# Counting ten one-hot columns: one VectorE sum in place of four additions

## The chip, the cores and the metric

The kernel runs on one core of one Trainium2 chip. The metric is the device time of one execution in microseconds. The engines are TensorE (PE), VectorE (DVE), ScalarE (ACT), GpSimd (POOL), and SyncE (SP), which issues plain DMAs.

## What is computed

One block of a graph transformer over N = 6250 rows of 256 values, with E = 106250 weighted edges. In the reference, cut to what matters:

```python
xn = layernorm(x)
low  = relu(segment_sum(val_low[:, None]  * (xn @ W_low)[dst],  src, N))   # GNN, two edge weights
high = relu(segment_sum(val_high[:, None] * (xn @ W_high)[dst], src, N))
mlp  = relu(xn @ W_mlp)
x = x + 3 * attention_mix(low, high, mlp) + linear_attention_mixer(xn)
y = layernorm(x);  weights = y @ wr
x = x + y + (ffn(y) * weights on the 3124 rows of largest weight, else 0)
```

The segment sum needs the edges grouped by `src`. The kernel does a counting sort of its own on the chip, into 98 buckets of 64 rows each (`src >> 6`), and this sort is where the change lies.

## The kernel before

Three stages follow one another. **The sort** (some 30 us to 765 us of the execution) takes the edges in 28 batches of 30 columns by 128 partitions, and runs beside it, tile quad by tile quad, the layer norm and key/value sums (slots 0 to 12), a folding of weights (slot 13), and the mixer (slots 14 to 24, with two quads left for after the last batch). **The gather stage** (some 765 us to 1835 us) fetches for every sorted column of 128 edges the rows of `xn` (852 indirect DMAs from GpSimd, line 665), multiplies them by selection matrices on TensorE, and runs attention, second layer norm and feed-forward tile by tile. **The end** finds the threshold of the largest weights and stores.

Every engine has its own instruction stream, all written out in the same order by `schedule` (line 372 on), which calls a function `slot(g, ...)` of each engine once a slot. Between engines there are semaphores only. In slot g VectorE does, in this order: the variance of the quad before; `pick_rank(g)` (line 766: 30 x 98 products of one-hots and ranks) and `place(g)` (lines 776 and 778 to 790: positions); key/value scaling, or in the mixer's slots `mix_out`; `one_hot(g+1)` (line 733: `oh`, for each of 128 partitions 30 columns of 98 buckets, bf16); `sum_hots(g+1)` (lines 746 to 752, the part that is changed); `cells(g)` and `cell_records(g)` (lines 794 to 808: operands of the permuting matmuls); layer-norm moments; `destinations(g-1)` (lines 824 and 826: where the records of batch g-1 go); `find_ties(g+1)`; `step_mask(g)`; the layer norm's apply.

`oh` is laid out [30 columns][98 buckets], so one column's 98 one-hots are contiguous and the same bucket of the next column lies 98 bf16 values, 196 bytes, further. The 30 columns make 3 groups of 10. `sum_hots` counts, in each partition and group, how many of the ten columns fall into each bucket: 3 x 98 counts. It does so by halves: columns 0-4 plus 5-9, then two plus two, then one plus one, then the odd fifth. Each addition waits for the one before through the semaphore `many_set`.

The counts go to TensorE's `ranks(g+1)`, its last work in slot g: it waits for `many_set` and for `idx_ready` of batch g-1, and multiplies the counts by triangles of ones into ranks. ScalarE copies these (`copy_rank`, line 1310), and VectorE's `pick_rank(g+1)` waits for that copy at the head of the next slot. GpSimd's `scatter(g)` (line 648) waits for `rec_staged` of ScalarE and for `idx_ready`, which line 826 on VectorE sets, and issues 16 indirect DMAs for the batch; index and record buffers are double, so VectorE's line 824 and ScalarE's line 1319 wait for the scatter of two batches before. The gather stage begins once all scatters have landed. Of the tile `many`, only `many[:, :, 0, :]` is read by TensorE.

Of the kernel before, what the change touches and what calls it, by code (L numbers as in the profile page):

```python
# [17 lines left out]
BF16 = mybir.dt.bfloat16  # L18
ALU = mybir.AluOpType
ACT = mybir.ActivationFunctionType  # L20
AX = mybir.AxisListType

P = 128
# [5 lines left out]
GS = 10  # L29
GROUPS = BB // GS  # L30
# [13 lines left out]
def wait(eng, sem, value):  # L44

    if isinstance(value, int) and value <= 0:
        return
    eng.wait_ge(sem, value)


def build(nc, a, out):
# [5 lines left out]
    NB = 2 * T  # L57
# [41 lines left out]
    with ExitStack() as ctx:  # L99
        sems = {}  # L100

        def S(name):
            if name not in sems:
                sems[name] = ctx.enter_context(nc.semaphore(name))
            return sems[name]

        def sb(name, shape, dt=F32):
            return ctx.enter_context(nc.sbuf_tensor(name, shape, dt))
# [37 lines left out]
        r1 = Region(0)  # L146
# [14 lines left out]
        oh = r1.take([P, BB, NB], BF16)  # L161
# [7 lines left out]
        quots = [base[:, spare:T * D].rearrange("p (j q) -> p j q", q=P), side[:, spare:T * D].rearrange("p (j q) -> p j q", q=P),  # L169
                 r1.take([P, GS, P])]  # L170
        iota_q = r1.take([P, STEPS], U16)
        many = r1.take([P, GROUPS, GS // 2, NB], BF16)
        iota32 = r1.take([P, P])
        earlier = r1.take([P, GS, GS], BF16)
        before_f = r1.take([P, P])
# [144 lines left out]
        ones_b = sb("ones_b", [P, P], BF16)  # L320
        before = sb("before", [P, P], BF16)
# [354 lines left out]
        def _(dve):  # L676
# [62 lines left out]
            def sum_hots(g):  # L739

                dve.wait_ge(S("oh_set"), g + 1)
                wait(dve, S("rank_ready"), g)
                h = oh[:, :, :].rearrange("p (s j) b -> p s j b", s=GROUPS)
                H = GS // 2
                with nc.allow_low_precision(reason="whole numbers up to ten"):
                    dve.tensor_tensor(many[:, :, :, :], h[:, :, 0:H], h[:, :, H:GS], ALU.add).then_inc(S("many_set"), 1)
                    dve.wait_ge(S("many_set"), 4 * g + 1)
                    dve.tensor_tensor(many[:, :, 0:2], many[:, :, 0:2], many[:, :, 2:4], ALU.add).then_inc(S("many_set"), 1)
                    dve.wait_ge(S("many_set"), 4 * g + 2)
                    dve.tensor_tensor(many[:, :, 0], many[:, :, 0], many[:, :, 1], ALU.add).then_inc(S("many_set"), 1)  # L750
                    dve.wait_ge(S("many_set"), 4 * g + 3)
                    dve.tensor_tensor(many[:, :, 0], many[:, :, 0], many[:, :, 4], ALU.add).then_inc(S("many_set"), 1)

            def find_ties(g):

# [14 lines left out]
            def place(g, par):  # L770

                dve.wait_ge(S("prod_set"), g + 1)
                dve.wait_ge(S("ties_set"), g + 1)
                H = (NB + GS) // 2
                with nc.allow_low_precision(reason="whole numbers below 2 ** 13, one of a bucket's and at most nine ties"):
                    dve.tensor_tensor(prod[:, :, 0:H], prod[:, :, 0:H], prod[:, :, H:2 * H], ALU.add).then_inc(S("prod_half"), 1)
                    dve.wait_ge(S("prod_half"), g + 1)
                    dve.tensor_reduce(posi[:, :], prod[:, :, 0:H], AX.X, ALU.add).then_inc(S("pos_set"), 1)
                dve.wait_ge(S("pos_set"), g + 1)
# [117 lines left out]
            def slot(g, par, kv, ln, post, mix, mixed):  # L897
# [15 lines left out]
                if more:  # L913
                    one_hot(g + 1)
                    sum_hots(g + 1)
# [125 lines left out]
            dve.tensor_reduce(hcnt[0:M, :, :].rearrange("p b k -> p (b k)"), hsel[0:M, :, :], AX.X, ALU.add).then_inc(S("hist_split"), 1)  # L1041
            one_hot(0)
            sum_hots(0)
            dve.wait_ge(S("counts_ready"), 1)
            step(dve.tensor_copy(cnt_i[0:NR, :], bank[6][0:NR, 0:G]))
# [234 lines left out]
            for n, (t0, t1) in enumerate(OUT):  # L1280
                if n == 0:
                    dve.wait_ge(S("y_ready"), t1)
                    for i in range(t0, t1):
                        ins = dve.scalar_tensor_tensor(base[:, i * D:(i + 1) * D], side[:, i * D:(i + 1) * D], mask[:, i:i + 1],
                                                       base[:, i * D:(i + 1) * D], ALU.mult, ALU.add)
                else:
                    dve.wait_ge(S("y_masked"), n)
                    ins = dve.tensor_tensor(base[:, t0 * D:t1 * D], base[:, t0 * D:t1 * D], side[:, t0 * D:t1 * D], ALU.add)  # L1288
# [234 lines left out]
        def _(pe):  # L1523
            def mm(out_, lhsT, rhs, start, stop, **kw):
                return pe.matmul(out_, lhsT, rhs, start=start, stop=stop, **kw)  # L1525


            def ranks(g):

                pe.wait_ge(S("many_set"), 4 * g + 4)  # L1530
                wait(pe, S("idx_ready"), 1 if isinstance(g, int) and g == 1 else g - 1)
                R = bank[0][:, 0:RANKS]
                mm(R, ones_f[0:NB, :], diag[0:NB, :].unsqueeze(1).to_broadcast([NB, GROUPS, NB]), True, False, skip_group_check=True)
                mm(R, before[:, :], many[:, :, 0, :], False, False, skip_group_check=True)
                for s in range(GROUPS - 1):
                    ins = mm(R[:, (s + 1) * NB:], ones_b[:, :], many[:, s:s + 1, 0, :].to_broadcast([P, GROUPS - 1 - s, NB]),
                             False, s == GROUPS - 2, skip_group_check=True)
                ins.then_inc(S("rank_ready"), 1)

# [3 lines left out]
            for g in range(G):  # L1543
                if g % (G // 2) == 0:
                    pe.wait_ge(S("digits_ready"), (H1 + H2) * (1 + g // (G // 2)))
                for u in range(BB // HG):
                    c = g * (BB // HG) + u
                    ins = mm(bank[2 + g // PER][0:M, (g % PER) * W:(g % PER + 1) * W], oh1[:, c * M:(c + 1) * M], oh2[:, c * W:(c + 1) * W],
                             u == 0, u == BB // HG - 1)
# [3 lines left out]
            for k in range(H2):  # L1553
                ins = mm(bank[6][0:NR, 0:G], spread[0:M, k, :, :].rearrange("p h k -> p (h k)"), hcnt[0:M, :, k], k == 0, k == H2 - 1)
            ins.then_inc(S("counts_ready"), 1)
            pe.wait_ge(S("runs_ready"), 1)
            mm(bank[6][0:NR, 32:32 + G], before_f[0:NR, 0:NR], runs[0:NR, :], True, True).then_inc(S("lpos_ready"), 1)
            pe.wait_ge(S("diag_ready"), 1)
            ranks(0)
            pe.wait_ge(S("totals_ready"), 1)  # L1560
            mm(bank[6][0:NR, 64:65], before_f[0:NR, 0:NR], incl[0:NR, G - 1:G], True, True)
# [123 lines left out]
            def slot(g, par, kv, ln, post, mix, mixed):  # L1685
# [53 lines left out]
                if more:  # L1739
                    ranks(g + 1)  # L1740
# [12 lines left out]
            for k in range(NBLK):  # L1753
# [6 lines left out]
                for f in range(4):  # L1760
                    ins = pe.transpose(bank[k][:, f * P:f * P + n], by_field[:, f, :], ident[0:n, 0:n])
# [151 lines left out]
```

## Time and profile before

| | us |
|---|---|
| median of 3 runs | 1971.31 (1970.63 to 1973.62) |
| the profiled execution's own time | 1968.29 |
| its span in the profile | 1966.5 |
| VectorE busy in the span | 1239.8 (63%) |
| GpSimd busy | 1376.8 (70%) |
| TensorE matmul busy | 1567.2 (80%) |

Busy time is the sum of instruction durations on an engine. Line numbers are those of the kernel. In a row of the timeline the first number is the start, the second the duration, and a bracket at the end says how long the engine sat idle before it and who ended that. An instruction's recorded duration can overlap by some tens of nanoseconds with the next one on its engine that does not wait for it, so what a step costs its engine is read from start to start.

### The profile page before, as it was taken

How to read it: one execution, taken by the hardware profiler on the slowest of the kernel's cores; microseconds unless marked ns; L12 is line 12 of the kernel's file. 1: busy time of each engine (PE TensorE's matmuls, PEld its weight loads, DVE VectorE, ACT ScalarE, POOL GpSimd, SP SyncE). 2: the span in 40 equal slices, each digit the busy share in tenths (PEclk: the TensorE clock that was granted, in tenths of full speed). 3: DMA queues.
4: the chain of work that ended last, by engine and by line, in shares of the span. 5: the costliest groups of instructions: out<-in, count | busy, mean ns of one | idle time of the engine just before them, and what ended most of it. 6: DMA issues, size and time to landing. Idle time of an engine off the chain costs nothing.

```text
span 1966.5 us, 30490 instructions
## 1 busy us (share of the span) xinstructions
PE 1567.2 (80%) x9109; PEld 1327.7 (68%) x9109; DVE 1239.8 (63%) x3136; ACT 915.6 (47%) x2641; POOL 1376.8 (70%) x1351
## 2 busy tenths in 40 slices
PE   3788888599998561788889888888888888889871
PEld 3466666588877561577777777777777777777750
DVE  8899999879988730345544554455454545545546
ACT  1688888677877550133333343333333334333323
POOL 4337778777777776777777777777777777777700
PEclk9899999789999785799999999999999999999975
DMA  3222221111121003433333333333333333333303
GB/s 89 83 66 68 68 68 49 40 36 47 48 66 47 6 6 95 133 102 105 100 102 103 104 101 105 105 101 100 102 103 103 102 103 105 100 102 105 103 14 131
DMA packets 102212, 162.99 MB, mean 83 GB/s; under 512 B 32190, under 2 KB 72762, under 8 KB 102040
## 3 DMA queue, kind: packets, MB, share of 16 engines
q0 software_dynamic: 55232, 113.59, 20.6%
q1 hardware_dynamic: 46808, 47.29, 7.6%
q8 instruction: 85, 1.39, 0.3%
q14 instruction: 87, 0.71, 0.1%
HBM read 139.76 MB, written 21.04 MB: 82 GB/s over the span
## 4 chain that ended last, share of the span: by engine, by line
POOL 31%; issue 13%; DMA 9%; DVE 2%; PE 2%; SPq 2%; ACT 1%; DVEq 0%; POOLq 0%; ACTq 0%
POOL arena L665 31%; DMA arena<-xn_rows,arena 9%; PE bank L1525 2%; SPq L558 1%; ACT side L1516 1%; POOL sorted_records L648 1%; DVE arena L1246 0%; DVE arena L1248 0%; DVE arena L1119 0%; DVE arena L1113 0%; SPq L563 0%; SPq L561 0%; DVE base L1288 0%; DVE arena L1253 0%; DVE arena L1245 0%
## 5 line engine op out<-in xcount | busy, mean ns | idle before, releaser
L1525 PE MATMUL bank<-arena 128*128 128x128 f32 (+3 forms) x6320 | 1145.1, 338 | 146.8 <-DVE arena L1119 74.4
L1525 PEld LDWEIGHTS bank<-arena 128*128 128x128 f32 (+1 forms) x6320 | 982.5, 188 | 287.8 <-issue 143.2
L665 POOL DMA_INDIRECT arena<-xn_rows,arena x852 | 840.7, 987 | 267.1 <-issue 246.1
L648 POOL DMA_INDIRECT sorted_records<-arena x448 | 512.9, 1145 | 218.0 <-issue 138.0
L1119 DVE TENSOR_TENSOR arena<-arena 128x640 f32<-128x640 bf16 (+1 forms) x204 | 164.4, 806 | 29.1 <-DVE arena L1113 0.2
L1113 DVE SCALAR_TENSOR_TENSOR arena<-io,arena 128x320 bf16<-128x320 f32 (+1 forms) x204 | 97.6, 479 | 96.5 <-issue 44.4
L1164 DVE CUSTOM_DVE_ANT_0 arena<-arena 128x256 f32<-128x256 f32 x98 | 37.8, 423 | 166.2 <-ACT arena L1449 166.2
L1169 DVE SCALAR_TENSOR_TENSOR att_prod<-sg,att_neg 128x9 f32<-128x9 f32 x49 | 8.4, 171 | 212.0 <-ACT sg L1457 212.0
L1525 PE MATMUL bank<-arena,base 128*128 128x128 f32 (+3 forms) x766 | 118.0, 287 | 22.0 <-ACT base L1304 13.8
L1525 PEld LDWEIGHTS bank<-arena,base 128*128 128x128 f32 (+2 forms) x766 | 110.2, 212 | 23.2 <-ACT base L1304 14.4
L1487 ACT ACTIVATE arena<-bank 128x256 f32<-128x256 f32 x49 | 18.8, 383 | 228.6 <-PE bank L1525 228.6
L808 DVE TENSOR_TENSOR arena<-arena 128x1280 f32<-128x1280 bf16 x84 | 120.3, 1488 | 1.0
L1435 ACT ACTIVATE arena<-bank,b1f 128x128 f32<-128x128 f32 x392 | 106.1, 385 | 5.0 <-PE bank L1525 5.0
L1465 ACT ACTIVATE nr<-nri 128x1 f32<-128x1 f32 x49 | 9.9, 203 | 203.1 <-DVE nri L1194 203.1
L1525 PE MATMUL bank<-side,arena 128*128 128x512 f32 x196 | 100.9, 641 | 0.0
L1300 ACT ACTIVATE base<-arena 128x128 f32<-128x128 f32 x280 | 84.8, 388 | 19.3 <-DVE arena L789 19.3
L1300 ACT ACTIVATE arena<-arena 128x128 f32<-128x128 f32 x280 | 84.7, 399 | 0.0
L1300 ACT ACTIVATE side<-arena 128x128 f32<-128x128 f32 x280 | 84.6, 395 | 0.0
L1449 ACT ACTIVATE arena<-bank 128x512 f32<-128x512 f32 x49 | 29.3, 597 | 102.2 <-PE bank L1525 102.2
L1440 ACT ACTIVATE arena<-bank 128x256 f32<-128x256 f32 x49 | 18.8, 383 | 123.9 <-PE bank L1525 123.9
L1525 PE MATMUL bank<-arena,side 128*128 128x128 f32 x560 | 67.7, 276 | 0.1
L766 DVE TENSOR_TENSOR arena<-arena 128x2940 f16<-128x2940 bf16 x28 | 47.3, 1689 | 32.0 <-ACT arena L1310 31.9
(311 smaller groups left out, 1918.2 us busy)
## 6 DMA issues: line engine op xcount, KB each, us to landing
arena<-xn_rows,arena POOLq DMA_INDIRECT x852
sorted_records<-arena POOLq DMA_INDIRECT x448
arena<-in_x SPq DMA_DIRECT2D x12, 512.0 KB, 4.1
xn_rows<-arena SPq DMA_DIRECT2D x12, 512.0 KB
x_plus_xn_rows<-arena SPq DMA_DIRECT2D x12, 512.0 KB
arena<-x_plus_xn_rows SPq DMA_DIRECT2D x12, 512.0 KB, 3.9
arena<-xn_rows SPq DMA_DIRECT2D x12, 512.0 KB
out<-base SPq DMA_DIRECT2D x4, 1024.0 KB
```

What stands on the lines that cost most here:

```text
L558: word = sp.value_load(free_word[group:group + 1, 0:1], min_val=1, max_val=2 ** 19 - 1)
L648: pool.indirect_dma_start(rec_dram, bass.IndirectOffsetOnAxis(ap=idx[0:PR, par, u:u + 1], axis=0), stage_rec[0:PR, par, u * 8:(u + 1) * 8] ...
L665: pool.indirect_dma_start(gring[:, c % GR, :], None, xn_dram, bass.IndirectOffsetOnAxis(ap=rring[:, c, 3:4].bitcast(I32), axis=0)).then_in ...
L766: dve.tensor_tensor(prod4[:, :, :, 0:NB], oh[:, :, :].rearrange("p (s j) b -> p s j b", s=GROUPS), rankf[:, :].rearrange("p (s b) -> p s b ...
L808: dve.tensor_tensor(cellrec[:, t, :].rearrange("p t (f c) -> p t f c", f=4), cell[:, t, :].unsqueeze(2).to_broadcast([P, GS, 4, GC]), raw[ ...
L1113: return dve.scalar_tensor_tensor(out_, io64[:, :].unsqueeze(1).to_broadcast([P, n, BK]), float(BK * b), r[:, :, 0:1].to_broadcast([P, n, ...
L1119: return dve.tensor_tensor(out_, hots.unsqueeze(2).to_broadcast([P, n, 2, BK]), r[:, :, 1:3].unsqueeze(3).to_broadcast([P, n, 2, BK]), ALU ...
L1164: ins = dve.tensor_tensor_reduce(out=lg_prod[:, k, :], in0=lh[:, k * D:(k + 1) * D], in1=att_rows[:, k, :], scale=1.0, scalar=0.0, op0=ALU ...
L1300: ins = act.activation(quot[:, j, :], iota32[:, :], ACT.Abs, bias=p32[:, par, s * GS + j:s * GS + j + 1], scale=-1.0)
L1435: act.activation(fh[:, f, :], bank[4 + part][:, (f % 4) * P:(f % 4 + 1) * P], ACT.Gelu_apprx_tanh, bias=b1f[:, f:f + 1]).then_inc(S("fh_re ...
L1449: act.activation(lh[:, :], bank[3][:, :], ACT.Relu).then_inc(S("lh_ready"), 1)
L1525: return pe.matmul(out_, lhsT, rhs, start=start, stop=stop, **kw)
```

## The change

The four additions of `sum_hots` become one `tensor_reduce` over a view of `oh` whose innermost axis runs along the ten columns of a group. The tile `many` shrinks to the 3 x 98 counts, and TensorE's `ranks` reads it directly and waits for one increment a batch where there were four. All 28 batches are changed. Nothing else is; the layer-normed rows are computed on VectorE as before.

```diff
--- before.py
+++ after.py
@@ -169,7 +169,7 @@
         quots = [base[:, spare:T * D].rearrange("p (j q) -> p j q", q=P), side[:, spare:T * D].rearrange("p (j q) -> p j q", q=P),
                  r1.take([P, GS, P])]
         iota_q = r1.take([P, STEPS], U16)
-        many = r1.take([P, GROUPS, GS // 2, NB], BF16)
+        many = r1.take([P, GROUPS, NB], BF16)
         iota32 = r1.take([P, P])
         earlier = r1.take([P, GS, GS], BF16)
         before_f = r1.take([P, P])
@@ -740,16 +740,8 @@
 
                 dve.wait_ge(S("oh_set"), g + 1)
                 wait(dve, S("rank_ready"), g)
-                h = oh[:, :, :].rearrange("p (s j) b -> p s j b", s=GROUPS)
-                H = GS // 2
                 with nc.allow_low_precision(reason="whole numbers up to ten"):
-                    dve.tensor_tensor(many[:, :, :, :], h[:, :, 0:H], h[:, :, H:GS], ALU.add).then_inc(S("many_set"), 1)
-                    dve.wait_ge(S("many_set"), 4 * g + 1)
-                    dve.tensor_tensor(many[:, :, 0:2], many[:, :, 0:2], many[:, :, 2:4], ALU.add).then_inc(S("many_set"), 1)
-                    dve.wait_ge(S("many_set"), 4 * g + 2)
-                    dve.tensor_tensor(many[:, :, 0], many[:, :, 0], many[:, :, 1], ALU.add).then_inc(S("many_set"), 1)
-                    dve.wait_ge(S("many_set"), 4 * g + 3)
-                    dve.tensor_tensor(many[:, :, 0], many[:, :, 0], many[:, :, 4], ALU.add).then_inc(S("many_set"), 1)
+                    dve.tensor_reduce(many[:, :, :], oh[:, :, :].rearrange("p (s j) b -> p s b j", s=GROUPS), AX.X, ALU.add).then_inc(S("many_set"), 1)
 
             def find_ties(g):
 
@@ -1527,13 +1519,13 @@
 
             def ranks(g):
 
-                pe.wait_ge(S("many_set"), 4 * g + 4)
+                pe.wait_ge(S("many_set"), g + 1)
                 wait(pe, S("idx_ready"), 1 if isinstance(g, int) and g == 1 else g - 1)
                 R = bank[0][:, 0:RANKS]
                 mm(R, ones_f[0:NB, :], diag[0:NB, :].unsqueeze(1).to_broadcast([NB, GROUPS, NB]), True, False, skip_group_check=True)
-                mm(R, before[:, :], many[:, :, 0, :], False, False, skip_group_check=True)
+                mm(R, before[:, :], many[:, :, :], False, False, skip_group_check=True)
                 for s in range(GROUPS - 1):
-                    ins = mm(R[:, (s + 1) * NB:], ones_b[:, :], many[:, s:s + 1, 0, :].to_broadcast([P, GROUPS - 1 - s, NB]),
+                    ins = mm(R[:, (s + 1) * NB:], ones_b[:, :], many[:, s:s + 1, :].to_broadcast([P, GROUPS - 1 - s, NB]),
                              False, s == GROUPS - 2, skip_group_check=True)
                 ins.then_inc(S("rank_ready"), 1)
 
```

## Rows read from the trace of the kernel before

**Rows 1.** The page, parts 1, 2 and 4.

```profile
PE 1567.2 (80%) x9109; PEld 1327.7 (68%) x9109; DVE 1239.8 (63%) x3136; ACT 915.6 (47%) x2641; POOL 1376.8 (70%) x1351
...
DVE  8899999879988730345544554455454545545546
...
POOL 4337778777777776777777777777777777777700
...
POOL 31%; issue 13%; DMA 9%; DVE 2%; PE 2%; SPq 2%; ACT 1%; DVEq 0%; POOLq 0%; ACTq 0%
```

**Rows 2.** Windows: one batch of each half (stretch, length, busy time per engine).

```profile
299.91:324.43 24.52, 21.99 (x145) 17.13 (x144) 23.79 (x50) 20.29 (x54) 19.64 (x17) 0.93 0.17 50
489.23:509.59 20.36, 20.15 (x145) 17.98 (x145) 19.65 (x30) 17.20 (x44) 16.09 (x15) 1.00 0.20 56
```

**Rows 3.** Timeline of VectorE (start, us taken): the four additions and what follows.

```profile
309.44 0.92 DVE L746 TENSOR_TENSOR arena<-arena 128x1470 bf16<-128x1470 bf16 x1
310.40 0.47 DVE L748 TENSOR_TENSOR arena<-arena 128x588 bf16<-128x588 bf16 x1
310.90 0.31 DVE L750 TENSOR_TENSOR arena<-arena 128x294 bf16<-128x294 bf16 x1
311.25 0.32 DVE L752 TENSOR_TENSOR arena<-arena 128x294 bf16<-128x294 bf16 x1
311.48 0.21 DVE L794 CAST arena<-arena 128x60 bf16<-128x60 int32 x1
```

**Rows 4.** Instructions by line on VectorE, whole trace: busy us, mean ns.

```profile
L778 DVE TENSOR_REDUCE arena<-arena 128x30 int32<-128x1620 f16 x28 | 51.6, 1841 | 1.0
...
L746 DVE TENSOR_TENSOR arena<-arena 128x1470 bf16<-128x1470 bf16 x28 | 26.2, 935 | 1.0
...
L1248 DVE TENSOR_REDUCE arena<-arena 128x15 f32<-128x735 f32 x8 | 7.4, 919 | 0.3
```

**Rows 5.** Timeline of VectorE: two sums of one tile, strided and contiguous.

```profile
17.82 0.29 DVE L707 TENSOR_REDUCE base<-base 128x6 f32<-128x78 f32 x1
18.03 0.23 DVE L708 TENSOR_REDUCE base<-base 128x13 f32<-128x78 f32 x1
```

**Rows 6.** Instructions of line 711, VectorE: ns min/median/max, starts, forms.

```profile
L711 DVE COPY base<-base x8: 163/168/566, 18.3 to 19.4; 128x12 f32<-128x12 f32 x6, 128x13 f32<-128x13 f32 x2
```

**Rows 7.** Timeline of VectorE: batch 0, first addition and what follows the fourth.

```profile
30.83 1.21 DVE L746 TENSOR_TENSOR arena<-arena 128x1470 bf16<-128x1470 bf16 x1
...
34.27 0.18 DVE L1045 CAST base<-bank 104x28 int32<-104x28 f32 x1
```

**Rows 8.** Timeline of VectorE: the products by rank, and the idle time before them.

```profile
299.91 1.68 DVE L766 TENSOR_TENSOR arena<-arena 128x2940 f16<-128x2940 bf16 x1
...
385.13 0.92 DVE L746 TENSOR_TENSOR arena<-arena 128x1470 bf16<-128x1470 bf16 x1
...
402.49 1.69 DVE L766 TENSOR_TENSOR arena<-arena 128x2940 f16<-128x2940 bf16 x1 [0.92 <-ACT arena L1310]
...
424.64 1.69 DVE L766 TENSOR_TENSOR arena<-arena 128x2940 f16<-128x2940 bf16 x1 [5.78 <-ACT arena L1310]
...
509.59 1.69 DVE L766 TENSOR_TENSOR arena<-arena 128x2940 f16<-128x2940 bf16 x1 [0.23 <-ACT arena L1310]
```

**Rows 9.** Timeline of VectorE and GpSimd: the handover of batch 14.

```profile
443.20 0.17 DVE L826 TENSOR_TENSOR arena<-arena,bank 128x16 int32<-128x16 f32 x1
...
444.17 1.43 POOL L648 DMA_INDIRECT sorted_records<-arena  x1 [3.06 <-DVE arena L826]
```

**Rows 10.** Windows of line 648 alone (scatters on GpSimd).

```profile
444.00:765.40 321.40, 248.75 (x224) 0.88 0.14 37
...
720.00:765.00 45.00, 34.33 (x36) 0.73 0.13 27
```

**Rows 11.** Timeline of VectorE: slot 26, which has no mixer work.

```profile
669.58 1.69 DVE L766 TENSOR_TENSOR arena<-arena 128x2940 f16<-128x2940 bf16 x1 [2.96 <-ACT arena L1310]
...
684.18 0.17 DVE L824 TENSOR_TENSOR arena<-bank,arena 128x16 f32<-128x16 f32 x1
```


## The prediction, made before the changed kernel ran

> **What bounds the kernel now.** I read the page first, for which stage the change touches and who is busy in it. The 40 slices are of 49 us each: VectorE stands at 8 or 9 tenths from the first slice to the tenth, the sort, and near half afterwards, where the chain that ended last is made mostly of GpSimd's gathers [rows 1]. The change is in the sort alone, and the gathers wait for its last scatter. So the question is what moves that scatter.
>
> Next I read two stretches of one batch each [rows 2]. In the first half of the sort a batch takes 24.52 us and VectorE has 23.79 of them; the rest is starts, not waiting: the timeline shows no idle bracket before its instructions. It is the bound. In the second half a batch takes 20.36 us and VectorE has 19.65; the one wait is 0.23 us at the head of the slot for ScalarE's copy of the ranks [rows 8]. TensorE has 20.15 us there, but its `ranks` waits for line 826 of VectorE, so the ring runs VectorE, TensorE, ScalarE, VectorE, and a longer VectorE slot makes the ring longer. From batch 14 on a third party counts. GpSimd waits 3.06 us for line 826 of VectorE and starts at 444.17 [rows 9]; from there to 765.4 it issues 224 scatters, 14 batches, 22.96 us each [rows 10]. That is slower than VectorE's 20.36, so VectorE gets ahead and GpSimd sets the end.
>
> In short: up to 443 us every microsecond on VectorE moves the end by one. After that only what makes its slot longer than about 23 us does.
>
> **What it removes.** The four additions take 2.04 us of VectorE, from the start of the first (309.44) to the start of line 794 (311.48), their waits on each other included [rows 3]. In batch 0 they take 3.44 us, 30.83 to 34.27, since some are slower there [rows 7].
>
> **What it adds.** One sum over 2940 bf16 values with 294 results. Two sums over contiguous values give the rate: 1620 values take 1841 ns and 735 take 919 ns, so (1841 - 919) / 885 = 1.042 ns a value and 153 ns fixed. The first of them reads f16, so 16-bit values bring no double rate in this row. An addition of 1470 bf16 values takes 935 ns, about half a nanosecond a value over the same fixed part [rows 4]. The floor for the sum is therefore 2940 x 1.042 + 153 = 3.22 us.
>
> But those rows step from one value to its neighbour. Here the innermost step is 196 bytes. One pair of rows in the trace shows what a step can cost: lines 707 and 708 sum the same 78 f32 values, 707 with an innermost step of 24 bytes and 708 along the row: 293 ns against 226 [rows 5]. The 67 ns are 0.86 ns a value, nearly one more tick of 1.042 ns each. In line 711, which writes 12 values at a step of 32 bytes, the median is 168 ns, only some 15 ns over the fixed part of the sums [rows 6]; this speaks neither for nor against a price on reads. I take the row of the same operation. Scaled by values, 2940 x 0.86 = 2.53 us more, 5.75 us in all. If a full tick is added to each value and the short sum hid its first dozen, it is 2940 x 2.084 + 153 = 6.28 us. Floor 3.22, ceiling 6.28; I take 6.0, between the two readings of the nearest row. Like line 752 it overlaps its successor by 0.09 us [rows 3], so it costs 5.91 from start to start, and a batch gets **5.91 - 2.04 = 3.87 us** longer on VectorE.
>
> The Trainium skill, SBUF — State Buffer, section "Door 1: The DMA port swizzle", says that SBUF is read in lines of 16 bytes and that each access which crosses to a new line pays a penalty. The trace agrees as far as it goes, by the 67 ns of line 707; the page gives no price.
>
> **Edits at no cost.** TensorE reads the counts from 294 contiguous values where it read three runs of 98; it has the same columns, and one semaphore count a batch in place of four costs VectorE only what the 2.04 us already contain. No DMA, no queue and no PSUM bank is touched. GpSimd's scatters take 1.11 us each while VectorE works (248.75 / 224) and 0.95 us in the last stretch with hardly any (34.33 / 36) [rows 10], 2.5 us a batch for all of VectorE's work. If the additions had their share, 2.04 of 20 us, their absence would give GpSimd back 0.26 us a batch, 3.6 us over 14 batches; what the sum takes from it instead is unknown. I count zero and keep 4 us either way.
>
> **Where the 3.87 us land.** Behind the sum on VectorE stand lines 794 to 808, whose cells TensorE permutes in the next slot, and lines 824 and 826, for which both TensorE's `ranks` and GpSimd wait.
> - Batch 0: 5.91 - 3.44 = +2.5 us, before anything overlaps it.
> - The sums of batches 1 to 14, the last at 385.13 [rows 8]: 14 x 3.87 = +54.2 us. The weight folding in slot 13 is a dialogue of VectorE and TensorE and is only moved.
> - The sum in slot 14 (402.49 to 424.64): VectorE idles 5.78 us before the next batch's products [rows 8], for TensorE's mixer work. This covers 3.87 us: 0. Without that cover it would be one more 3.87.
> - The sum in slot 15 stands ahead of line 826 at 443.20, for which GpSimd waits [rows 9]: +3.9 us. Batch 14 is handed over 60.6 us later, at 503.8.
> - From slot 16 VectorE needs 20.36 + 3.87 = 24.23 us a batch, GpSimd 22.96. So GpSimd waits for VectorE again. To line 826 of slot 26 there are 11 slots, the last 3.8 us shorter (14.60 us from line 766 to 824 [rows 11], where in slots with mixer work three more instructions, 3.8 us, come between): 11 x 24.23 - 3.8 = 262.7, batch 25 at 766.5, GpSimd's start 1 us later, 767.5.
> - Batches 25 to 27 are then GpSimd's again: with VectorE thinning out, between 20.0 us (45.00 / 36 x 16) and 22.96 us each [rows 10], 65.5 us for the three. The last scatter ends at 833.0 where it ended at 765.4.
>
> The gather stage and the end move as they are. Sum: **+67.6 us** on the profiled execution's 1968.3, which gives 2035.9. That execution stands 3.0 us under the median of the runs shown, so I predict 1971.3 + 67.6 = **2039 us**. With a sum of 5.75 us the same steps give +61 to +62 (2033), with 6.28 us +75 (2046).
>
> **Rivals.**
> *The step costs nothing.* Then the sum takes 3.22, a batch gets 3.13 - 2.04 = 1.09 us longer. Batch 0 gains 0.3, batches 1 to 14 lose 15.3, slot 15 loses 1.1; then the VectorE slot is 21.45 us, under GpSimd's 22.96, and after one more handover, which is just in time today, nothing is added: +17, **1988 us**. For it: line 711, and that the 67 ns are one single instruction. Against it: lines 708, 778 and 1248 lie within 10 ns of one line, 707 does not. The Trainium skill, VectorE: DVE Perf Modes, section "Mode 1× (REGULAR) — the baseline", has one result a cycle whatever the stride; by that rule this rival holds, and the 67 ns of line 707 contradict it here.
> *The sum reads bf16 in pairs.* The place is the sum itself: at two values a tick it takes 2940 x 0.521 + 153 = 1.69 us, 1.60 from start to start, 0.45 us under the additions. It decides for a gain once the sum is shorter than 2.13 us. 15 batches give back 6.7 us, batch 0 another 1.8, and GpSimd's pace swallows the rest: -8.5, **1963 us**. For it: the additions do read at that rate. Against: the f16 sum of line 778 does not, and pairs along a step of 196 bytes are not neighbours.
> *GpSimd covers it.* If its rate counted from the first batch, nothing would change (1971). Against: it waits for line 826 up to batch 14 [rows 9].
>
> **How the numbers follow.** The step costs: 0.70. It costs nothing: 0.23. Pairs: 0.05. Cover or a chance meeting near zero: 0.02. Against a measurement that can tell 0.2% (4 us): slower 0.93, same 0.02, faster 0.05. Range: the likeliest case runs from 2033 to 2046, with 4 us for GpSimd 2029 to 2050; to leave out no more than 2 in 10 it must reach down to the second case, less the 4 us: 1984 to 2050.
>
> **What will show it.** In the changed profile one sum of 2940 values on VectorE near 6.0 us (3.2: the first rival; under 2.1: the second). Batches of the first half 28.4 us apart at line 766. An idle time of GpSimd before each batch's scatter after 500 us, ended by line 826; about 1.9 us of idle time left before line 766 after slot 14. A last scatter near 833 us and a gather stage as long as before. I am wrong if the sum's duration is outside 5.7 to 6.3 us, or if the slots of the second half stretch by less than the sum does.

## The result and the profile after

| | before | changed |
|---|---|---|
| median, us | 1972.39 (1970.63 to 1973.62, 4 runs) | 2033.38 (2026.91 to 2035.38, 4 runs) |
| ratio | | 1.0304, 95% interval 1.0279 to 1.0329 |
| span of the profiled execution | 1966.5 | 2031.8 |
| last scatter issued (line 648) | 764.2 | 820.9 |
| first and last gather issued (line 665) | 771.5, 1872.1 | 828.3, 1938.1 |

The kernel is 61 us slower; forecast were 67 (2039, range 1984 to 2050). The page of the changed kernel, the lines that answer to [rows 1]:

```profile
PE 1593.4 (78%) x9109; PEld 1350.0 (66%) x9109; DVE 1327.7 (65%) x3052; ACT 915.4 (45%) x2641; POOL 1396.0 (69%) x1351
...
DVE  8899999989999991145544554554455545555446
...
POOL 31%; issue 12%; DMA 9%; DVE 2%; PE 2%; SPq 2%; ACT 1%; DVEq 0%; POOLq 0%; ACTq 0%
```

VectorE stands at 8 or 9 tenths in each of the first 15 slices, of 51 us now, where before, in slices of 49 us, it stood so in 12 of the first 13; it has 84 instructions fewer (3052 against 3136) and 88 us more work. The chain that ended last is GpSimd's as before.

The timeline of VectorE round one sum, which answers to [rows 3] (start, us taken), and below it all 28 sums of line 744 (ns min/median/max, first and last start):

```profile
342.62 5.25 DVE L744 TENSOR_REDUCE arena<-arena 128x294 bf16<-128x2940 bf16 x1
347.79 0.18 DVE L786 CAST arena<-arena 128x60 bf16<-128x60 int32 x1
```

```profile
L744 DVE TENSOR_REDUCE arena<-arena x28: 5067/5222/5294, 30.8 to 740.0; 128x294 bf16<-128x2940 bf16 x28
```

The sum takes 5.25 us here and 5.17 us from its start to the next start. The additions took 2.04. Batch 0, which answers to [rows 7]:

```profile
30.80 5.09 DVE L744 TENSOR_REDUCE arena<-arena 128x294 bf16<-128x2940 bf16 x1
...
35.80 0.19 DVE L1037 CAST base<-bank 104x28 int32<-104x28 f32 x1
```

5.00 us where it was 3.44: +1.6 us. Two stretches of one batch each, which answer to [rows 2] (stretch, length, busy time of PE, PEld, DVE, ACT, POOL):

```profile
332.91:360.53 27.62, 23.22 (x145) 18.59 (x144) 27.00 (x47) 20.15 (x54) 19.35 (x17) 0.87 0.15 45
518.90:542.31 23.41, 21.78 (x146) 19.59 (x147) 22.80 (x26) 17.14 (x44) 18.53 (x17) 0.94 0.17 49
```

In the first half a batch takes 27.62 us, 3.10 more than 24.52, which is the sum's 5.2 less 0.1 overlap less 2.04. In the second half it takes 23.41, 3.05 more than 20.36. So all of the sum's extra time lengthens the slots in both halves. Not every slot of the second half takes 23.4 us; some take 24.2, and the part on why the prediction was right comes back to them. The handover of batch 14, line 818 being line 826 of before; VectorE first, GpSimd after it ([rows 9] before):

```profile
490.17 0.17 DVE L818 TENSOR_TENSOR arena<-arena,bank 128x16 int32<-128x16 f32 x1
...
491.13 1.43 POOL L648 DMA_INDIRECT sorted_records<-arena  x1 [1.65 <-DVE arena L818]
...
518.07 1.44 POOL L648 DMA_INDIRECT sorted_records<-arena  x1 [1.65 <-DVE arena L818]
```

Line 818 runs at 490.17 where it ran at 443.20: **47.0 us later**. GpSimd waits 1.65 us for it, once more before batch 15 at 518.07, and then not again: from there to the last scatter no idle time before a batch is longer than the 0.3 us that lies between any two of its instructions. Its 13 batches from 518.07 to the end of the last scatter at 821.9 take 23.4 us in the mean, but they are not alike: 23.4 to 24.3 us in the first six, 27.6 in the seventh (26.0 before), and 20.8 in the mean of the last three. The first and last issue of the scatters and of the gathers, with the durations in ns:

```profile
L648 POOL DMA_INDIRECT sorted_records<-arena x448: 954/958/2522, 66.0 to 820.9; - x150
...
L665 POOL DMA_INDIRECT arena<-xn_rows,arena x852: 942/946/1543, 828.3 to 1938.1; - x171
```

The last scatter comes 56.7 us later than before, and from first to last gather it is 1109.8 us where it was 1100.6. Of the 65.3 us between the two spans 47.0 are there at the handover of batch 14, 9.7 come between it and the last scatter, and 9.2 in the gather stage; what lies outside these comes to -0.6.

### The profile page after: what moved, and what is told of

It is laid out like the page before. It is cut to its first block, busy times and chain, and to the rows that moved or that the text cites. A ratio compares the mean times of both kernels' runs of the same rounds, so it can differ in the third digit from the quotient of the medians.

```text
span 2031.8 us, 30406 instructions
## 1 busy us (share of the span) xinstructions
PE 1593.4 (78%) x9109; PEld 1350.0 (66%) x9109; DVE 1327.7 (65%) x3052; ACT 915.4 (45%) x2641; POOL 1396.0 (69%) x1351
## 4 chain that ended last, share of the span: by engine, by line
POOL 31%; issue 12%; DMA 9%; DVE 2%; PE 2%; SPq 2%; ACT 1%; DVEq 0%; POOLq 0%; ACTq 0%
POOL arena L665 30%; DMA arena<-xn_rows,arena 9%; PE bank L1517 2%; SPq L558 1%; ACT side L1508 1%; POOL sorted_records L648 1%; DVE arena L1238 0%; DVE arena L1240 0%; DVE arena L1111 0%; DVE arena L1105 0%; SPq L563 0%; SPq L561 0%; DVE base L1280 0%; DVE arena L1245 0%; DVE arena L1237 0%
## 5 line engine op out<-in xcount | busy, mean ns | idle before, releaser
L665 POOL DMA_INDIRECT arena<-xn_rows,arena x852 | 850.0, 998 | 267.2 <-issue 245.9
L648 POOL DMA_INDIRECT sorted_records<-arena x448 | 523.3, 1168 | 265.1 <-issue 134.2
L1517 PE MATMUL bank<-arena,base 128*128 128x128 f32 (+3 forms) x766 | 145.7, 336 | 18.8 <-DVE nr L975 11.1
L1517 PEld LDWEIGHTS bank<-arena,base 128*128 128x128 f32 (+2 forms) x766 | 136.5, 258 | 19.9 <-DVE nr L975 11.2
L744 DVE TENSOR_REDUCE arena<-arena 128x294 bf16<-128x2940 bf16 x28 | 145.9, 5209 | 1.0
L1517 PE MATMUL bank<-arena,ones_f 98*128 98x294 f32 (+2 forms) x74 | 34.4, 555 | 117.0 <-DVE arena L818 97.5
L1517 PEld LDWEIGHTS bank<-arena,ones_f 98*128 98x128 f32 (+2 forms) x74 | 15.0, 251 | 124.9 <-issue 102.8
L1517 PE MATMUL bank<-side,arena 128*128 128x512 f32 x196 | 95.3, 609 | 0.0
```

The source lines that it names most:

```text
L648: pool.indirect_dma_start(rec_dram, bass.IndirectOffsetOnAxis(ap=idx[0:PR, par, u:u + 1], axis=0), stage_rec[0:PR, par, u * 8:(u + 1) * 8] ...
L665: pool.indirect_dma_start(gring[:, c % GR, :], None, xn_dram, bass.IndirectOffsetOnAxis(ap=rring[:, c, 3:4].bitcast(I32), axis=0)).then_in ...
L744: dve.tensor_reduce(many[:, :, :], oh[:, :, :].rearrange("p (s j) b -> p s b j", s=GROUPS), AX.X, ALU.add).then_inc(S("many_set"), 1)
```

## The experiments

All runs below but sum_early_b and sum_late_b came out on four other chips, on which the kernel before took 2514 to 2558 us; they are called disturbed here. The difference is one of the chips and not of the kernel: a profile of the unchanged kernel on the first of them (before_again, TensorE and GpSimd from 900 to 2440 us, sum of waits, times, longest) shows TensorE waiting for its own instruction stream, "issue", for 448 us in the gather stage, where the first profile has 133, and GpSimd waiting 445 us for SyncE's queue, where it had 21:

```profile
PEld bank L1525 <- issue: 448.4, 307, 8.8
POOL arena L665 <- SPq L564: 444.7, 64, 12.8
```

The mean granted clock of TensorE is lower there too, 0.822 against 0.927, and its 9109 matmuls are busy for 1760.9 us where they took 1567.2. Which of these comes first is not shown. Whole times from these chips count for nothing below about 1%; single durations on VectorE are the same there (line 766 takes 1.69 us on both).

**What the step costs.** Thirteen extra sums in the kernel before, twice over, ahead of slot 1:

```diff
+ for r in (1, 2, 4, 8, 16, 32, 96):      # bf16 one-hots; then 1, 2, 4, 8, 96 on f32 records
+     tensor_reduce(out[:, 0:288], flat[:, 0:2880].rearrange("p (a j r) -> p a r j", j=10, r=r), AX.X, ALU.add)
+ tensor_reduce(many[:, :, 0, :], oh.rearrange("p (s j) b -> p s b j", s=3), AX.X, ALU.add)   # the sum of the change
```

> The kernel before, with two passes of thirteen extra sums on VectorE ahead of slot 1: twelve of 2880 values with 288 results whose innermost step is 2, 4, 8, 16, 32, 64 or 192 bytes (bf16, read from the one-hots) and 4, 8, 16, 32 or 384 bytes (f32), and the sum of the change itself (2940 bf16 values, 196 bytes). The results go to an unused part of the counts' tile and are not read. Theory (a step into another 16-byte line costs): 2880 x 1.042 + 153 = 3.15 us for bf16 steps of 2, 4 and 8 bytes and f32 steps of 4 and 8; from 16 bytes on about 5.1 us whatever the step, as the 5.21 us of the change's sum. Rival 1 (the price grows with the step, or comes from bank conflicts of the one step of 196 bytes): 64 and 192 bytes differ from 16 and 32, or only 196 is dear. Rival 2 (the price belongs to sums that do not read neighbours in order): already the 4-byte bf16 step costs 5 us.

Timeline of VectorE in that kernel. Lines 1107 to 1113 are bf16 with steps of 2, 4, 8, 16, 32, 64 and 192 bytes; 1114 to 1118 are f32 with steps of 4, 8, 16, 32 and 384 bytes; 1119 is the sum of the change:

```profile
69.69 3.14 DVE L1107 TENSOR_REDUCE arena<-arena 128x288 bf16<-128x2880 bf16 x1
72.86 3.15 DVE L1108 TENSOR_REDUCE arena<-arena 128x288 bf16<-128x2880 bf16 x1
76.05 3.15 DVE L1109 TENSOR_REDUCE arena<-arena 128x288 bf16<-128x2880 bf16 x1
79.24 5.27 DVE L1110 TENSOR_REDUCE arena<-arena 128x288 bf16<-128x2880 bf16 x1
84.54 5.28 DVE L1111 TENSOR_REDUCE arena<-arena 128x288 bf16<-128x2880 bf16 x1
89.86 4.95 DVE L1112 TENSOR_REDUCE arena<-arena 128x288 bf16<-128x2880 bf16 x1
94.84 4.96 DVE L1113 TENSOR_REDUCE arena<-arena 128x288 bf16<-128x2880 bf16 x1
99.84 3.15 DVE L1114 TENSOR_REDUCE arena<-arena 128x288 bf16<-128x2880 f32 x1
103.03 3.15 DVE L1115 TENSOR_REDUCE arena<-arena 128x288 bf16<-128x2880 f32 x1
106.22 5.09 DVE L1116 TENSOR_REDUCE arena<-arena 128x288 bf16<-128x2880 f32 x1
111.34 5.25 DVE L1117 TENSOR_REDUCE arena<-arena 128x288 bf16<-128x2880 f32 x1
116.63 4.98 DVE L1118 TENSOR_REDUCE arena<-arena 128x288 bf16<-128x2880 f32 x1
121.64 5.07 DVE L1119 TENSOR_REDUCE arena<-arena 128x294 bf16<-128x2940 bf16 x1
```

The second pass gave the same thirteen durations within 0.01 us. Steps up to 8 bytes take 3.15 us, whatever the type; from 16 bytes on it is 4.95 to 5.28 us for both types, and 196 bytes are nothing special. That is 1.8 to 2.1 us on 2880 values, 0.63 to 0.74 ns a value where one tick of the contiguous sum is 1.04 ns. The theory's figures came out and both rivals fall: the 4-byte step reads no neighbour and costs nothing, and the price does not grow with the step. Steps of 64 and 192 bytes do differ from 16 and 32, as the first rival had it, but they are 0.1 to 0.3 us cheaper, for which I have no cause. No step between 8 and 16 bytes was run, so the rows do not show whether the price begins with a new line of 16 bytes or with any step above 8. The Trainium skill, SBUF — State Buffer, section "Door 1: The DMA port swizzle", has a penalty for each access that crosses to a new line of 16 bytes, with which the rows agree; but the same note counts a stride of 4 f32 or 8 bf16 values as free, and these two, 16 bytes each, paid the whole price (5.09 and 5.27 us). What the price is, only these rows say.

**Where the sums cost, by batch.** One kernel with the sum in batches 0 to 14, one with it in batches 15 to 27, the additions in the others:

```diff
 def sum_hots(g):
+    if g <= 14:             # sum_late: g >= 15
+        dve.tensor_reduce(many[:, :, 0, :], oh[...].rearrange("p (s j) b -> p s b j", s=GROUPS), AX.X, ALU.add)
+        return
     ... four additions ...
```

> The sum in batches 0 to 14, the four additions in batches 15 to 27. Theory (VectorE is the bound up to the handover of batch 14, GpSimd after it): batch 14 is handed over about 44 us later than before (batch 0 +1.7, 14 batches of +3.1), after that GpSimd's pace of 22.96 us covers VectorE's 20.4 us slots, so the last scatter too comes about 44 us later: near 2016 us. Rival (each of the 28 sums costs the same share of the whole 61 us): 15/28 of it, 33 us, near 2005.

> The four additions in batches 0 to 14, the sum in batches 15 to 27. Theory: the sum of batch 15 is hidden under TensorE's mixer work, that of batch 16 moves the handover of batch 14 by 3.1 us, and from there VectorE's slots of 23.4 us are a little longer than GpSimd's 22.96 us: 10 slots x 0.5 us, some starts more, together +9 to +13 us: near 1983 us. Rival (GpSimd covers the second half entirely): +3 us, 1975. Rival (equal share): 13/28 of 61, +28 us, 2000.

On a disturbed chip: 2584.34 and 2547.29 us against 2558.23, ratios 1.0135 [1.0023, 1.0248] and 0.9943 [0.9897, 0.9990]. The second is hard to believe of a kernel that only adds work on VectorE, and in the profiles VectorE idles up to 10 us (sum_late) and up to 26 us (sum_early) ahead of single batches from slot 14 on. These two runs decide nothing. The same two kernels on a chip like the first:

> The kernel of sum_early again, since on the chip of the first series TensorE fell behind its own instruction stream and the kernel before took 2558 us there. With the kernel before at 1972 us, theory (GpSimd's pace covers VectorE after the handover of batch 14): the handover of batch 14 comes near 487 us (443.2 + 44), the last scatter 44 us later than before, the whole near 2016 us. Rival (each sum costs the same share): 2005 us.

> The kernel of sum_late again, for the same reason. Theory: batch 14 handed over 3.1 us later (446.3), VectorE's slots of 23.4 us from there on, last scatter +9 to +13 us: near 1983 us. Rival (GpSimd covers the second half entirely): 1975 us. Rival (equal share): 2000 us.

Here the kernel before took 1970.54 us. sum_early_b: **2018.58**, ratio 1.0245 [1.0228, 1.0262], +48.0 us. sum_late_b: **1985.51**, ratio 1.0076 [1.0060, 1.0093], +15.0 us. Together 63.0, and the whole change costs 61.0. Timeline of VectorE in sum_early_b (line 839 is the handover, 779 the products by rank) and all its scatters (line 656):

```profile
487.33 0.17 DVE L839 TENSOR_TENSOR arena<-arena,bank 128x16 int32<-128x16 f32 x1
...
513.00 1.69 DVE L779 TENSOR_TENSOR arena<-arena 128x2940 f16<-128x2940 bf16 x1 [0.22 <-ACT arena L1323]
...
533.36 1.69 DVE L779 TENSOR_TENSOR arena<-arena 128x2940 f16<-128x2940 bf16 x1 [0.22 <-ACT arena L1323]
```

```profile
L656 POOL DMA_INDIRECT sorted_records<-arena x448: 954/959/2525, 65.7 to 808.1; - x150
```

The handover comes at 487.33, 44.1 us later than before, for 487 expected. From there VectorE's slots are 20.36 us again, and the last scatter comes at 808.1, 43.9 us later: GpSimd keeps the delay and adds none. The same lines of sum_late_b:

```profile
446.16 0.17 DVE L839 TENSOR_TENSOR arena<-arena,bank 128x16 int32<-128x16 f32 x1
...
474.88 1.69 DVE L779 TENSOR_TENSOR arena<-arena 128x2940 f16<-128x2940 bf16 x1 [0.23 <-ACT arena L1323]
...
498.30 1.69 DVE L779 TENSOR_TENSOR arena<-arena 128x2940 f16<-128x2940 bf16 x1 [0.22 <-ACT arena L1323]
```

```profile
L656 POOL DMA_INDIRECT sorted_records<-arena x448: 952/959/2720, 62.8 to 777.0; - x150
```

Handover 3.0 us later, slots of 23.42 us, last scatter at 777.0: 12.8 us later than before, of which 9.8 after the handover. So GpSimd does not cover the second half, and the shares are not equal: 3.2 us a sum in the first fifteen batches by whole time, 1.2 us in the last thirteen. As 23.42 us is only 0.5 us over the 22.96 us a batch that GpSimd had before, most of the sum's 3.1 us is hidden there.

**The gather stage.** Its instructions are the same in all kernels. Two more profiles of the unchanged kernel were to tell whether its 9.2 us are chance:

> The kernel before unchanged, for a second profile. Asked of it: how much the gather stage (first to last gather of line 665: 1100.6 us in the profile of before, 1109.8 us in that of the changed kernel, which has the same instructions there) varies between executions of one program. Theory (the 9 us belong to how VectorE's work falls against GpSimd's in one execution): here it is between 1100 and 1112 us and need not be 1100.6. Rival (the change lengthens the gather stage, by another start or another placing of tiles): 1100 to 1102 us here.

> The kernel before unchanged, for a second profile on a chip like that of the first. First to last gather of line 665 took 1100.6 us in the profile of before and 1109.8, 1108.2 and 1108.1 us in those of the changed kernel, sum_early_b and sum_late_b, with the mean gather instruction at 987 ns against 996 to 998. Theory (the stage varies between executions, and the one profile of before was a quick one): 1103 to 1109 us here, and a mean above 990 ns. Rival (every kernel whose sort was changed has a longer gather stage, by where VectorE's work falls against GpSimd's): 1100 to 1102 us and 987 ns again.

Both fell on disturbed chips (2562.2 and 2574.15 us), where the stage takes over 1500 us; they tell nothing on it. What is there: the stage took 1100.6 us before and 1109.8, 1108.2 and 1108.1 in the three kernels with sums, and the difference is in the duration of GpSimd's own instructions. Lines on the scatters and gathers (busy us, mean ns, idle before), changed kernel first, then the kernel before:

```profile
L665 POOL DMA_INDIRECT arena<-xn_rows,arena x852 | 850.0, 998 | 267.2 <-issue 245.9 <-SPq L564 21.3
...
L648 POOL DMA_INDIRECT sorted_records<-arena x448 | 523.3, 1168 | 265.1 <-issue 134.2 <-DVE arena L818 95.1 <-ACT arena L1311 35.9
```

```profile
L665 POOL DMA_INDIRECT arena<-xn_rows,arena x852 | 840.7, 987 | 267.1 <-issue 246.1 <-SPq L564 21.0
...
L648 POOL DMA_INDIRECT sorted_records<-arena x448 | 512.9, 1145 | 218.0 <-issue 138.0 <-DVE arena L826 50.8 <-ACT arena L1319 29.3
```

852 x (998 - 987) ns = 9.4 us, with the same idle time before them. That this one profile of before was quick is plausible, as its execution took 1968.29 us, 4.1 us under the median of the four unprofiled ones, while that of the changed kernel, 2033.57, lies at its median; but no second profile shows it. It stays open how much of the 9 us belongs to the change.

**Taking work off VectorE instead.** If VectorE is the bound, the opposite edit should gain: leave the last two additions, or the last three, to TensorE.

```diff
 # pe_three: parts 0, 1, 4 of many are left; pe_five: parts 0 to 4
-mm(R, before[:, :], many[:, :, 0, :], ...)
+for k in (0, 1, 4):
+    mm(R, before[:, :], many[:, :, k, :], ...)
 for s in range(GROUPS - 1):
-    mm(R[:, (s + 1) * NB:], ones_b, many[:, s:s + 1, 0, :]...)
+    for k in (0, 1, 4):
+        mm(R[:, (s + 1) * NB:], ones_b, many[:, s:s + 1, k, :]...)
```

> The kernel before without the third and fourth addition: TensorE takes the three parts that are left, by nine matmuls with bf16 counts in place of three. VectorE loses 0.58 us a batch (from the start of line 750 to that of line 794), TensorE gains some 0.6 us. Theory (VectorE bounds up to the handover of batch 14, where GpSimd has 3.1 us of idle time left, and 1 us a batch in the first half): VectorE's slots in the first half go from 24.53 to 23.95 us, the handover comes 9 us earlier, but GpSimd can use only some 5 us of it: -3 to -9 us, near 1966. Rival (TensorE's ranks stand in the ring VectorE, TensorE, ScalarE, VectorE, so its 0.6 us take back what VectorE gives): 0.

> Only the first addition is left; TensorE takes five parts by fifteen matmuls. VectorE loses 1.1 us a batch, TensorE gains some 1.2 us. Theory: slots of the first half 23.4 us, where TensorE has then 23.2 us of work; GpSimd is saturated before the handover, so hardly more than the three-part kernel gives: -4 to -12 us. Rival: TensorE becomes the bound in the mixer's slots (20.15 us of 20.36 are its work now) and its slots pass 21.5 us; still under GpSimd's pace, so the time is that of the three-part kernel or worse by a few us.

> The kernel of pe_three again on a chip where the kernel before takes some 1972 us, if it is given one. Theory: handover of batch 14 up to 9 us earlier, of which GpSimd can use 3 to 5 us: -3 to -9 us, near 1966. Rival (the ring through TensorE takes it back): 0.

> The kernel of pe_five again, for the same reason. Theory: slots of the first half at TensorE's 23.2 us or more, GpSimd saturated before the handover: -4 to -12 us. Rival: TensorE the bound of the mixer's slots, slots past 21.5 us, nothing gained over the three-part kernel.

> The kernel of pe_three once more, beside a profile of the kernel before from the same chip. Theory: -3 to -9 us against the kernel before. Rival: 0. Its gather stage, by the two theories of before_again_b: 1103 to 1109 us, or about 1108 us because the sort was changed.

All five fell on disturbed chips. pe_three: ratios 1.0051 [1.0005, 1.0097], 1.0037 [1.0002, 1.0072] and 1.0051 [0.9999, 1.0104]. pe_five: 0.9952 [0.9899, 1.0006] and 1.0049 [1.0007, 1.0090]. No gain is shown. More matmuls on a chip whose TensorE is behind may well cost what the additions gave back, but these runs do not show that either. In the first half of the sort VectorE's slots do what was expected of them. Timeline of pe_five_b (line 760 the products by rank, 746 the one addition that is left, 788 what follows it):

```profile
147.72 1.68 DVE L760 TENSOR_TENSOR arena<-arena 128x2940 f16<-128x2940 bf16 x1
...
157.26 0.92 DVE L746 TENSOR_TENSOR arena<-arena 128x1470 bf16<-128x1470 bf16 x1
...
158.10 0.18 DVE L788 CAST arena<-arena 128x60 bf16<-128x60 int32 x1
...
171.10 1.68 DVE L760 TENSOR_TENSOR arena<-arena 128x2940 f16<-128x2940 bf16 x1
```

The addition and its successor are 0.84 us apart where four additions took 2.04, and the slot is 23.38 us where it was 24.52. Whether this gives time on an undisturbed chip was not found out.

## Why the prediction was right, and where not

**What bounds.** Right. In both halves the slot of VectorE grew by the whole of what the sum added (3.10 and 3.05 us), and the handover of batch 14 in sum_early_b, forecast from the measured sum, came to the microsecond. After that handover GpSimd decides as long as VectorE's slots are short: those of 20.36 us in sum_early_b add nothing to the last scatter.

**The price of the sum.** The sign, the cause and the choice of row were right, the size was not. 6.0 us were forecast, between 5.75 and 6.28, and the median is 5.22; by the prediction's own words a sum outside 5.7 to 6.3 us makes it wrong on this term. The step that failed is "Scaled by values, 2940 x 0.86": the 67 ns of line 707 [rows 5], one instruction over 78 values, were spread evenly over the values, and the ladder shows 0.63 to 0.74 ns a value in sums of 2880. At that rate 78 values make 49 to 58 of the 67 ns; what the rest is, one short instruction cannot tell. A tick for every value, my upper end, is excluded: that would be 6.28 us. So a batch got 3.1 us longer, not 3.87.

**The handover of batch 14.** Forecast +60.6 us, measured +47.0. With the measured sum the same steps give 1.6 (batch 0) + 14 x 3.1 + 0 + 3.1 = 48.1. The cover in slot 14 was there: VectorE's idle time before line 766 (758 now) fell from 5.78 us [rows 8] to 1.97, where 1.9 were forecast. That the two agree is luck: the shorter sum should have left 2.7 us, as it does in sum_late_b (2.59), and the slot itself came out 0.6 us shorter, as it did in sum_early_b, where no sum stands in it and 5.18 are left. From the timeline of the changed kernel:

```profile
468.54 1.69 DVE L758 TENSOR_TENSOR arena<-arena 128x2940 f16<-128x2940 bf16 x1 [1.97 <-ACT arena L1302]
```

**From there to the last scatter.** Forecast +7.0 us, measured +9.7, from slips that nearly cancel. The first slot after the handover was counted like the others, 24.23 us; it took 26.94 (490.17 to 517.11), as 3.5 us of other work on VectorE lie in it (443.20 to 467.08 before). The ten batches after it took GpSimd 241.6 us (518.07 to 759.66), where the chain of slots has 238.5: ten times 24.23, the last 3.8 us shorter. As the sum was 0.7 us shorter than the chain had it, that the two are so near is luck. The last three batches took 62.3 us (759.66 to 821.9), where 65.5 were forecast.

The idle time of GpSimd that I said would stand before each batch after 500 us is not there beyond batch 15, and yet GpSimd follows VectorE. VectorE, GpSimd and TensorE in two slots of the changed kernel:

```profile
563.59 1.10 POOL L648 DMA_INDIRECT sorted_records<-arena  x1 [0.31 <-issue]
563.98 0.17 DVE L818 TENSOR_TENSOR arena<-arena,bank 128x16 int32<-128x16 f32 x1
564.30 0.73 PE L1517 MATMUL bank<-arena,ones_f 98*128 98x294 f32 x2 [1.68 <-DVE arena L818]
565.77 1.70 DVE L758 TENSOR_TENSOR arena<-arena 128x2940 f16<-128x2940 bf16 x1 [0.23 <-ACT arena L1302]
...
587.00 1.10 POOL L648 DMA_INDIRECT sorted_records<-arena  x1 [0.31 <-issue]
587.39 0.17 DVE L818 TENSOR_TENSOR arena<-arena,bank 128x16 int32<-128x16 f32 x1
587.71 1.32 PE L1517 MATMUL bank<-arena,ones_f 98*128 98x294 f32 x2 [3.26 <-DVE arena L818]
590.00 1.69 DVE L758 TENSOR_TENSOR arena<-arena 128x2940 f16<-128x2940 bf16 x1 [1.04 <-ACT arena L1302]
```

The scatter in each of these pairs is the last of its batch. Line 818 runs 0.38 to 0.39 us after it has begun, in these two slots as in all six from batch 16 to batch 21, whether the slot is of 23.4 or of 24.2 us. GpSimd's batch has the length of VectorE's slot there; 22.96 us was not a pace of its own, and its scatters took 1168 ns in the mean where they took 1145. How VectorE holds it stands in the last section.

The rows also show where the slots of 24.2 us come from, which the prediction did not have. In the second pair TensorE had waited 3.26 us for line 818, and its two matmuls for the ranks take 1.32 us instead of 0.73: the granted clock is 0.50 from 587.7 to 589.6 us (1.2 GHz) and 1.00 from 564.3 to 565.6 (2.4 GHz). ScalarE's copy of the ranks comes later by as much, and VectorE idles 1.04 us in place of 0.23. It is so in every slot that ends with 1.04 us of idle time; in those with 0.23 TensorE had waited 1.7 us at most. In four slots of the kernel before, from 487 to 549 us, it had waited 0.2 us and the granted clock was 1.00.

**The gather stage.** "The gather stage and the end move as they are": in the profiles it did not, by 9.2 us. If the sort's share is taken from the profiles and the whole from the medians, 4.3 us are left for it (61.0 less 56.7), 4.1 in sum_early_b (48.0 less 43.9) and 2.2 in sum_late_b (15.0 less 12.8). That the 2033 us are nearer to the forecast than its parts is therefore in part luck: the sort gave 10.9 us less than the 67.6 forecast, and the gather stage some 4 that were not forecast.

**The rivals.** "The step costs nothing" is out: 3.15 us is the price of steps up to 8 bytes only. With it falls for this case the rule of the Trainium skill, VectorE: DVE Perf Modes, section "Mode 1× (REGULAR) — the baseline", of one result a cycle whatever the stride. "Pairs" is out too: even the contiguous bf16 sum takes 3.15 us, the rate of f32. "GpSimd covers it" holds for slots of VectorE below some 23 us after 443 us, and for nothing else here.

## What to carry to other kernels

Count values and the bytes between them, not instructions: one sum of 2940 values took 5.2 us where four additions with 2646 results took 2.04, because additions of bf16 neighbours run at about half a nanosecond a value, a sum at 1.04, and a sum whose innermost step is 16 bytes or more at about 1.7. Look for even one strided instruction in the trace before such a change; here it gave the sign, but its excess over a short tile overstated the rate of a long one. And where a second engine is slower than the bound one in part of the time, split the change by batch and run the halves: 48 and 15 us here told more than the whole.

## What was not expected of the hardware

- The price of a step is a cliff, not a slope: for 2880 values 3.15 us at 8 bytes, 5.09 (f32) and 5.27 (bf16) at 16, 5.25 and 5.28 at 32, and 4.95 to 4.98 from 64 bytes on.
- The same sum took between 5.07 and 5.29 us within one execution, the short ones at its start, in slot 13 and in the last batches (5.07 us also in both passes of the ladder), while a contiguous sum of the kernel (line 778, 1840 to 1842 ns in all 28 batches before) does not vary.
- GpSimd's indirect DMA instructions take 0.95 to 0.96 us or are held by a VectorE instruction, and then they end some 0.83 us after it. In the changed kernel from 520 to 680 us 31 of the 39 scatters that took over 1.05 us end within 0.03 us of that, and of the 68 shorter ones only one does. Among what holds them are the products of line 758, the comparisons of line 808 and, before the change, the addition of line 748. The sum does not: the 21 scatters that lie wholly inside a sum took 0.95 or 0.96 us. From the changed kernel, the sum of that slot being at 576.95 to 582.15:

```profile
578.05 0.95 POOL L648 DMA_INDIRECT sorted_records<-arena  x1 [0.30 <-issue]
...
588.21 0.75 DVE L808 TENSOR_SCALAR arena<-arena 99x2048 bf16<-99x2048 uint16 x1
588.41 1.38 POOL L648 DMA_INDIRECT sorted_records<-arena  x1 [0.30 <-issue]
...
590.09 2.43 POOL L648 DMA_INDIRECT sorted_records<-arena  x1 [0.30 <-issue]
```

588.41 + 1.38 is 0.83 after 588.96, the end of line 808, and 590.09 + 2.43 is 0.83 after 591.69, the end of line 758. A scatter that meets the same VectorE instruction in every slot is let go at the same place in every slot, which would keep the two engines in step as seen above; that this is the cause was not tested.
